# Transformer layers on one Trainium2 core: a loop body of two units in place of four, with values projected beside queries and keys

## What is computed

```python
def attn_layer(x, Wqkv, qs, ksc, Wo):        # x is shift_tokens(x)
    q, k, v = split(x @ Wqkv)                # 16 heads of 64
    q, k = rotary(l2norm(q) * qs), rotary(l2norm(k) * ksc)
    out = local_attention(q, k, v)           # window of 32 rows and the one before it
    return out @ Wo
def ffn_layer(x, g, bln, W1, b1, W2, b2):    # x is shift_tokens(x)
    a, gate = split((layernorm(x) * g + bln) @ W1 + b1)
    return a * gelu(gate) @ W2 + b2
for i in range(6):
    x = attn_layer(shift_tokens(x), ...) + x
    x = ffn_layer(shift_tokens(x), ...) + x
```

## Time and profile before

| | us |
|---|---|
| median of three runs | 3991.84 |
| lowest and highest | 3988.7, 3993.46 |
| the profiled execution | 3979.11 |
| its span, first to last instruction | 3977.3 |

### The profile page before, as it was taken

One profiled execution on the slowest core, in us unless ns is written; L12 is line 12 of the kernel. 1 busy time (PEld: TensorE's weight loads), 2 busy tenths in 40 slices (PEclk: granted clock), 3 DMA queues, 4 the chain that ended last, 5 costly groups with the idle time before them and its releaser, 6 DMA issues.

```text
span 3977.3 us, 158623 instructions
## 1 busy us (share of the span) xinstructions
PE 3528.5 (89%) x60708; PEld 2531.4 (64%) x60708; DVE 3481.0 (88%) x7219; ACT 2616.5 (66%) x4783; POOL 2522.5 (63%) x2671
## 2 busy tenths in 40 slices
PE   6887799998998989989989989989989889899997
PEld 3444476666666666666666666666666666666665
DVE  7888898998898988889989988889889889888895
ACT  3445676776676766667767676666667667666675
POOL 3334576766666766666667666666667667666673
PEclk9878899999999999999999999999999999999998
DMA  2000111112211112211111211112211112211112
GB/s 66 5 5 4 25 49 44 48 44 54 66 42 50 42 49 55 59 50 42 50 42 54 67 42 50 42 42 67 53 47 45 47 45 60 61 42 45 47 44 60
DMA packets 126086, 184.83 MB, mean 46 GB/s; under 512 B 26742, under 2 KB 49332, under 8 KB 124724
## 3 DMA queue, kind: packets, MB, share of 16 engines
q1 hardware_dynamic: 125492, 175.28, 17.2%
HBM read 21.32 MB, written 2.10 MB: 6 GB/s over the span
## 4 chain that ended last, share of the span: by engine, by line
PE 53%; ACT 21%; issue 20%; DVE 4%; ACTq 1%; POOL 0%; DMA 0%; DVEq 0%; SPq 0%; POOLq 0%
PE bank L1066 13%; PE bank L1210 10%; PE bank L1089 9%; PE bank L1152 6%; ACT L615 6%; ACT oT L574 4%; ACT gl L623 4%; PE bank L1167 4%; PE bank L972 2%; ACT znT L612 2%; ACT L626 2%; ACT vt L568 2%; PE bank L1144 2%; PE bank L1013 1%; PE bank L1120 1%
## 5 line engine op out<-in xcount | busy, mean ns | idle before, releaser
L436 POOL TENSOR_TENSOR qk<-ta,tb 128x512 f32<-128x512 f32 x768 | 971.6, 1275 | 513.3 <-DVE tb L814 513.3
L552 ACT ACTIVATE sq<-bank 128x512 f32<-128x512 f32 x768 | 459.3, 598 | 777.9 <-PE bank L1066 771.2
L1066 PE MATMUL bank<-wqkv,zsT 128*128 128x512 f32 x1536 | 831.1, 624 | 114.0 <-issue 104.9
L445 POOL TENSOR_TENSOR qk<-qk,rn 128x512 f32<-128x512 f32 x768 | 776.5, 1042 | 72.9 <-DVE rn L841 72.9
L814 DVE TENSOR_TENSOR ta<-bank,rot 128x512 f32<-128x512 f32 x768 | 529.4, 689 | 259.5 <-ACT sq L552 259.3
L478 POOL TENSOR_TENSOR P<-P,rowsum 128x512 f32<-128x512 f32 x384 | 393.6, 1044 | 498.9 <-DVE rowsum L930 498.9
L814 DVE TENSOR_TENSOR tb<-bank,rot 128x512 f32<-128x512 f32 x768 | 523.0, 681 | 0.0
L1089 PEld LDWEIGHTS bank<-cst,qk 128*128 128x128 f32 x3072 | 376.4, 146 | 214.4 <-issue 213.6
L1210 PE MATMUL bank<-wo,oT 128*128 128x128 f32 x3072 | 393.6, 281 | 130.3 <-ACT oT L574 130.2
L1210 PEld LDWEIGHTS bank<-wo,oT 128*128 128x128 f32 x3072 | 357.4, 191 | 167.1 <-ACT oT L574 128.5
L926 DVE TENSOR_REDUCE ss<-sq 128x32 f32<-128x2048 f32 x192 | 437.0, 2276 | 0.0
(11 more groups left out here) (135 smaller groups left out, 6924.6 us busy)
## 6 DMA issues: line engine op xcount, KB each, us to landing
vs<-vt SPq DMA_DIRECT2D x1152, 128.0 KB, 2.4
wqkv<-L_ffn_Wqkv SPq DMA_DIRECT2D x6, 1024.0 KB, 4.9
wqkv<-L_ffn_Wqkv SPq DMA_DIRECT2D x6, 512.0 KB, 3.8
wo<-L_ffn_Wo SPq DMA_DIRECT2D x6, 512.0 KB, 4.2
z_sb<-x SPq DMA_DIRECT2D x4, 512.0 KB, 6.8
ctxb<-ctx SPq DMA_DIRECT2D x32, 64.0 KB, 1.7
out<-x_sb SPq DMA_DIRECT2D x8, 256.0 KB, 3.5
w<-L_ffn_W SPq DMA_DIRECT2D x6, 341.0 KB, 3.0
```

The costliest lines, as they stand in the source:

```text
L436: g.tensor_tensor(o, i0, i1, ALU.add).then_inc(s["g_add"], 1)
L445: g.tensor_tensor(q3, q3, r3, ALU.mult).then_inc(s["g_qk"], 1)
L552: a_.activation(sq[:, 512 * j:512 * j + 512], bank[j % 2][:, :], ACT.Square)\
L1066: t_.matmul(bank[j % 2][:, :], zsT[:, k % 4, :], wqkv[:, 512 * j:512 * j + 512], start=True, stop=True).then_inc(s["p_qk"], 1)
```

## The change

The loop body holds two slots in place of four (UNROLL 2), and `zsT` has two buffers. To make that possible, the values of a unit are projected in the slot of its queries and keys. The output product y moves from the end of a slot to the next slot's head, behind transposes 0 and 1, and the second feed-forward product y2 with it, for the unit `f` = n-5. On PE, PT now stands ahead of the scores, and zT behind them; on ScalarE the copies of zsT stand behind those of PT. VectorE's list has a new order: z_sb of unit f behind root(2), zm behind root(4), the sum of squares ahead of the row sum, and the reciprocal at the very end. GpSimd does two of its four normalizations ahead of `add(1)`. There is one more slot at the end. SP's copies of v and weight loads are put in an order that fits.

```diff
-        zsT = sb("zsT", [128, 4, S])
+        zsT = sb("zsT", [128, 2, S])
...
-        LOOP0, UNROLL = 8, 4
-        LOOP1 = UNITS - 4
+        LOOP0, UNROLL = 6, 2
+        LOOP1 = UNITS - 2
...
-            for n in range(LOOP1, UNITS + 4):
+            for n in range(LOOP1, UNITS + 5):
...
 # SP
-                first = B * layer + 2
+                start, end = B * layer, B * layer + B
                 if layer == 0:
-                    shift_v(0, 0)
-                    shift_v(1, 1)
+                    for u in range(3):
+                        shift_v(u, u % 2)
...
 # POOL
+                if m_on:
+                    normalize(0)
+                    normalize(1)
                 if a_on:
                     add(1)
                 if m_on:
-                    for j in range(4):
-                        normalize(j)
+                    normalize(2)
+                    normalize(3)
...
 # ACT
-                    wait(act, "p_v", count(2, b, e + 1))
-                    wait(act, f"l_v{pb}", ...)
-                    a_.activation(vt[:, pb, e, :], bank[e][:, :], ACT.Copy)
+                    wait(act, "p_v", count(2, a, e + 1))
+                    wait(act, f"l_v{pa}", ...)
+                    a_.activation(vt[:, pa, e, :], bank[e][:, :], ACT.Copy)
...
 # DVE
                 if m_on:
                     root(0)
+                    root(1)
+                if a_on:
+                    rotary(0)
+                if m_on:
+                    root(2)
+                if f_on:
+                    wait(dve, "p_y2", count(1, f, 1))
+                    wait(dve, "g_zmb", count(1, f, 1))
+                    v_.tensor_tensor(z_sb[:, cols(f)], bank[6][:, 384:512], zmb[:, pf, :], ALU.add)
+                if m_on:
+                    root(3)
+                    root(4)
                 if d_on:
                     wait(dve, "p_y", count(1, d, 1))
...
-                if b_on:
-                    wait(dve, "a_exp", count(1, b, 1))
-                    wait(dve, "g_P", count(2, b - 1, 2))
-                    v_.tensor_reduce(rowsum[:, 0, :], ...)
                 if a_on:
                     wait(dve, "a_sq", count(4, a, 4))
...
                     v_.tensor_reduce(ss[:, pa, :], ...)
                 if b_on:
+                    wait(dve, "a_exp", count(1, b, 1))
+                    wait(dve, "d_rec", count(1, b - 1, 1))
+                    v_.tensor_reduce(rowsum[:, 0, :], ...)
                     wait(dve, "d_sum", count(1, b, 1))
+                    wait(dve, "g_P", count(2, b - 1, 2))
                     v_.reciprocal(rowsum[:, 1, :], rowsum[:, 0, :])
...
 # PE, the new head of a slot
+                if a_on:
+                    proj_qk(0)
+                if b_on:
+                    transpose_qk(0)
+                    transpose_qk(1)
+                if f_on:
+                    wait(pe, "d_h", count(1, f, 1))
+                    for j, (_, m) in enumerate(FCH):
+                        ins = t_.matmul(bank[6][:, 384:512], hT[0:m, j, :], w2[0:m, j, :], ...)
+                if d_on:
+                    wait(pe, "a_AV", count(2, d, 2))
+                    for p in range(PAIRS):
+                        ins = t_.matmul(bank[7][:, 384:512], oT[:, p, :], wo[:, 2 * (p % 4) + p // 4, :], ...)
+                if a_on:
+                    proj_qk(1)
+                if d_on:
+                    wait(pe, "d_zm", count(1, d, 1))
...
                     for j in range(2):
                         wait(pe, "g_P", count(2, c, j + 1))
-                        edge(pe, n, "a_tr", count(4, b, 4))
+                        wait(pe, "a_tr", count(4, b, j + 3))
...
+                if b_on:
+                    scores()
+                if z_on:
+                    wait(pe, "g_z", count(1, zu, 1))
...
-                    t_.matmul(bank[r][:, :], zsT[:, (k + 2) % 4, :], wv[:, :, r, :], start=True, stop=True)
+                    t_.matmul(bank[r][:, :], zsT[:, k % 2, :], wv[:, :, r, :], start=True, stop=True)
```

More of the change, by code:

```diff
@@ L344, in _ @@
             for layer in range(DEPTH):
-                first = B * layer + 2
+                start, end = B * layer, B * layer + B
                 if layer == 0:
-                    shift_v(0, 0)
-                    shift_v(1, 1)
+                    for u in range(3):
+                        shift_v(u, u % 2)
                 with sp.Fori(0, (B - 6) // 2) as i:
                     for k in range(2):
-                        shift_v(i * 2 + (first + k), k)
-                shift_v(B * layer + B - 4, 0)
+                        shift_v(i * 2 + (start + 3 + k), (3 + k) % 2)
+                shift_v(end - 3, 1)
                 if layer + 1 < DEPTH:
                     load_qk(layer + 1)
-                for k in range(3):
-                    shift_v(B * layer + B - 3 + k, (1 + k) % 2)
+                shift_v(end - 2, 0)
                 if layer + 1 < DEPTH:
                     load_v(layer + 1)
-                    shift_v(B * layer + B, 0)
+                shift_v(end - 1, 1)
+                if layer + 1 < DEPTH:
+                    shift_v(end, 0)
+                    shift_v(end + 1, 1)
                     load_o(layer + 1)
-                    shift_v(B * layer + B + 1, 1)
+                    shift_v(end + 2, 0)
                     load_ffn(layer + 1)
@@ L545, in slot @@
                 d, d_on = part(n, 4)
[L546 removed]
+                pa, pb = k % 2, k % 2
                 def square(j):
@@ L589, in slot @@
                     square(2)
[L590 to L599, removed]
                 if c_on:
@@ L606, in slot @@
                                       ACT.Copy).then_inc(s["a_PT"], 1)
+                if z_on:
+                    wait(act, "p_zT", count(1, zu, 1))
+                    wait(act, "p_v", count(2, zu - 2, 2))
+                    if isinstance(zu, int) and zu < 2:
+                        wait(act, "u_zs", 1)
+                    t = zsT[:, (k + 1) % 2, :]
+                    a_.activation(t[0:64, :], bank[7][0:64, 0:128], ACT.Copy).then_inc(s["a_zs"], 1)
+                    a_.activation(t[64:128, 1:128], bank[7][64:128, 0:127], ACT.Copy).then_inc(s["a_zs"], 1)
                 if d_on:
@@ L853, in slot @@
                 if m_on:
[L854 to L858, removed]
+                    root(5)
+                    root(6)
                 if d_on:
@@ L863, in slot @@
                 if m_on:
-                    root(3)
+                    root(7)
                 if d_on:
@@ L870, in slot @@
                 if m_on:
-                    root(4)
+                    root(8)
                 if d_on:
@@ L928, in slot @@
                 if b_on:
+                    wait(dve, "a_exp", count(1, b, 1))
+                    wait(dve, "d_rec", count(1, b - 1, 1))
+                    v_.tensor_reduce(rowsum[:, 0, :], P[:, pb, :].rearrange("p (h t) -> p h t", t=DH), AX.X, ALU.add)\
+                        .then_inc(s["d_sum"], 1)
                     wait(dve, "d_sum", count(1, b, 1))
+                    wait(dve, "g_P", count(2, b - 1, 2))
                     v_.reciprocal(rowsum[:, 1, :], rowsum[:, 0, :]).then_inc(s["d_rec"], 1)
[L931 to L936, removed]
             slots(dve, slot)
@@ L1050, in slot @@
                 d, d_on = part(n, 4)
+                f, f_on = part(n, 5)
                 pb, pc, pd = k % 2, (k - 3) % 2, k % 2
```

85 lines of the change are left out of this document (37 added, 48 removed).

## The result

| | before, us | changed, us |
|---|---|---|
| median of the runs | 3992.65 | 4154.2 |
| lowest, highest | 3988.7, 4025.35 | 4145.11, 4157.14 |
| profiled execution | 3979.11 | 4157.14 |
| its span | 3977.3 | 4155.3 |

The change makes the kernel slower: ratio 1.038, interval 1.0325 to 1.0439. The prediction of 3932 was wrong in size and in sign, and the time lies 64 us outside its range.

What follows compares the result with a forecast made beforehand. It took y's wait for ScalarE's oT copies and PE's code rereading in the loop as the bounds. 3977.3 - 214 + 159 = 3922, 3924 with 1.8 around it, plus 8 for spread: 3932 us, range 3790 to 4090.

Steps and rivals of the forecast that it cites:

- (d): VectorE's new order: the cycle through a later zm makes a slot 18.0 us, 0.85 longer, +159 us over 187 slots.
- What bounds the kernel before: Slots of 17.15 us, where y waits 0.78 us for ScalarE's oT copies, and a loop losing 4.75 us a body.
- the loss of the loop: At the turn and inside the body of four, PE rereading its code: 4.75 us a body, 214 us in all.
- (a): Loop body of two: PE holds its code, the branch costs 0.2 us and the whole loop loss goes, -214 us.
- (b): y and y2 at the slot's head: the 0.78 us wait for oT goes; DVE's zm is late next.
- (c): Values projected in the slot of their unit: same matmuls and copies, no cost.
- The lump of 0.3: In the slot's cycle, 0.3 us allowed for four handovers between engines, bringing 17.71 to 18.0 us.
- The second rival: At DVE's slot head, POOL's pair catches root(0) too: 1.0 us later each body or slot, 4016 to 4111 us; chance 0.17.
- The first rival: DVE does not bind: slots of 17.15 us or less, 3765 us in all; chance 0.15.
- the third: PE's body of two is not held: branch 3.8 us, 92 times, gaps inside remain, 4100 us; chance 0.15.
- (e): PT ahead of the scores, waiting for transpose copies 2 and 3: no cost, at worst 0.3 us a slot.
- (f): One more slot at the end, holding only y2: less than 3 us, the front loses as much, so zero.

Runs made afterwards that it cites:

- e4: The kernel before with only values projected in the slot of their queries and keys and a loop body of two: 3826.88 us, ratio 0.960.
- e5: The kernel before with values projected in the slot of their queries and keys, loop body kept at four: 4003.18 us, ratio 1.004.
- e3: The changed kernel with a loop body of four slots in place of two: 4139.22 us, ratio 1.039.
- e2: The changed kernel with root(0) moved from the head of a slot to the end of the one before: 4027.66 us, ratio 1.011.

## Why the prediction was wrong, point by point

The step that failed is the price of the new order, +159 us in (d). Counted the same way, from a slot of 17.15 us, it was 393: 1.38 us in each of 187 slots in place of 0.85 (258 us), 0.99 us more at each turn (90 us), for which the sum had nothing, and the slow clock (45 us), for which it had nothing either.

**What bounds the kernel before: right.** e4 keeps the wait for oT. Its distance to e5, 176 us, bears out the loss of the loop, 214 in the sum: e5 too loses 4.7 us a body against four of its quietest slots (17.27), 212 us, and e4 wins back all but the 0.22 us by which its slots are longer than these.

**(a) The body of two: right.** Branch 208 ns, 28 fetches. The value taken, 0.2, was the right end of the bound. The Trainium skill, "Runtime: NRT & Kernel Launch", section Instruction fetch mechanics, has both a buffer of 2,048 instructions for PE and a window of two pages for a taken branch. The trace agrees with the first and not with the second: a body of 1,232 matmuls and loads is held, one of twice that is not. (A slot has 308 matmuls; the prediction's 316 come from all 60,708 over 192 units, the cross attention's among them.)

**(b) y at the head: right** that its wait goes, and that zm is late next. PE's idle before zsh is 1.41 us, the sum had 1.2.

**(c) Early values: right within the noise** (e5: ratio 1.004, interval across 1). The 0.12 us a slot that e5's trace has more, early values and no-op together, would be 22 us.

**(d) The new order: the mechanism was right and its size was not.** The same way, in the quiet slot shown above, from rotary(3) at 2140.80 to rotary(3) at 2159.24:

| leg | sum of the prediction | measured |
|---|---|---|
| rotary(3) to reciprocal | 5.42 | 5.51 |
| reciprocal to the end of zm | 4.46 | 4.62 |
| end of zm to the zT result | 4.94 | 5.28 |
| ScalarE, to the end of square(3) | 2.89 | 3.00 |
| handovers | 0.30 | 0.03 |
| in all | 18.01 | 18.44 |

The locks came where the sum had them: over the loop root(1) takes 0.92 us on average, root(3) 1.22 and root(7) 0.18, and root(3) ends 4.00 us after the start of the reciprocal, as predicted. Yet every leg is 0.1 to 0.3 us longer than its rows, because the handovers lie inside the measured legs, as the 0.11 us between root(4) and zm, or the 0.13 us from zm to PE. What fills each of these gaps isn't shown. The lump of 0.3 was too small by 0.4. With a mean of 18.53 over all slots of this kind that is 0.53 x 187 = 99 us.

**The turn: a rival that came true in part.** The second rival had the right mechanism, place and price (root(0) more than 0.32 us behind the reciprocal, 1.0 us, "in each body (92 us)"). It got 0.17, because I held that the sequencer runs ahead of a waiting instruction. It does not get past a reciprocal that waits: in each of the 92 bodies the first register instruction of the loop starts 0.014 us after the reciprocal has started, and root(0) follows 0.49 us (median) after that start. The kernel before had hidden this. There the row sum had ended before the sum of squares, so the reciprocal had nothing left to wait for, and the branch ran 0.30 us after the start of the sum of squares, 1.9 us ahead of the reciprocal. The rival and the forecast are not exclusive, though I priced them as if they were: both the longer slot and the catch at the turn came.

**A term that was missing.** PE's idle was counted as slack that costs nothing. Behind an idle of 2.3 us the clock stood at 0.50 for 3.4 us in 27 of 91 turns, 45 us. The trace of the kernel before had 28 such stretches in its loop, 22 at the idle of 2.2 to 2.7 us before qk0 behind a turn and 6 at a gap of 1.9 to 2.2 us in the scores. What they cost lies inside the 214 us that the sum gave back whole. One of them, as a stretch and on PE:

```profile
686.40:689.80 3.40, 3.12 (x8) 1.98 (x9) 0.14 (x1) 0.75 (x2) 0.03 (x1) 0.50 0.17 49
```
```profile
686.68 2.07 PE L1066 MATMUL bank<-wqkv,zsT 128*128 128x512 f32 x2 [2.42 <-issue]
```

So for the profiled execution 3924 + 99 + 90 + 45 = 4158 against 4157; the 8 us that were added for the spread of the runs did not come. The first rival (0.15) and the third (0.15) did not happen, and the sign hung on 60 us between -214 and +159: an error of 0.3 us in a slot of 18 was enough to turn it, and the range for it, 0.25 us to either side, was too narrow.

**(e), (f)**: no wait before PT shows in the slots quoted; the tail grew by about 5 us.

## What to carry to other kernels

When a step is taken out of the critical cycle, look for the next step that the same engine waits for, and put what feeds it first in its producer's list: here one small sum behind a blocked operation turned a gain of 5% into a loss of 4%. A sum of a cycle made from durations came out short here by 0.7 us in 18 before the lump for handovers, and by 0.4 us with it; such an error, multiplied by the number of slots, has to stand beside the gain before a sign is given. Two engines that meet within 0.1 us can fall either way (e3), and the price of both ways belongs in the range.

## What the runs showed of the hardware

- DVE operations of 0.12 to 0.19 us on SBUF operands, when they start while a POOL operation runs, last until it ends: root(0) 0.93, root(1) 0.99, root(3) 1.17 us. At a turn root(0) ends between the two POOL operations that follow each other, and root(1) meets the second. With a start 0.02 us ahead of POOL root(1) took 0.18 us (e3).
- PE holds a loop body of two slots (1,232 matmuls and loads; branch 208 ns, 28 fetches over the run), not one of four (3,765 to 4,427 ns, 571 fetches).
- A taken branch of 56 ns on DVE came with 0.49 us between the start of the instruction before it and the start of the one behind it. Where the instruction before it had to wait, the branch's register work began only with its start.
- PE's granted clock fell to 0.50, the 1.2 GHz level, for 3.4 us behind an idle of 2.3 us, in 27 of 91 such places (25 on another chip); in all 44 of e3, behind idles of 3.3 to 4.0 us, for 3.4 or 6.8 us; and in none of e2's slots, where the longest of these idles was 1.5 us. Why it falls in some of the equal slots and not in all is open.
